# The attention output kept by feature: small transfers in place of transpositions, in a decoder block with self and cross attention

## The reference

```
x1 = LN(h);  q,k,v = x1 @ Wqkv + b;  a = softmax(causal(q k^T / 4)) v;  h = h + a @ Wp1 + b
x2 = LN(h);  q = x2 @ Wq2 + b;  k,v = ctx @ Wkv2 + b
             a = softmax(q k^T / 4 + logits[key] + mask(key > query + 2)) v;  h = h + a @ Wp2 + b
x3 = LN(h);  h = h + gelu_tanh(x3 @ Wfc + b) @ Wmlp + b          (inner width 1024)
```

## Time and profile before

| | us |
|---|---|
| median of 3 runs | 1323.19 (1321.65 to 1323.44) |
| profiled execution, its time | 1324.19 |
| profiled execution, its span | 1322.5 |
| PE busy in the span | 1116.2 (84%) |
| DVE busy | 786.8 (59%) |
| ACT busy | 614.5 (46%) |
| POOL busy | 434.6 (33%) |
| one transfer queue, share of 16 engines' span | 40.0% |
| mean granted TensorE clock | 0.933 |

### The profile page before, as it was taken

The page is one execution under the profiler, slowest core; times in us unless marked ns, Lnnn a source line. Parts: engine busy times, 40 slices in busy tenths (PEclk is TensorE's granted clock), DMA queues, the critical chain, the costliest instruction groups (busy, mean ns, idle before and its releaser), DMA issues.

```text
span 1322.5 us, 22082 instructions
## 1 busy us (share of the span) xinstructions
PE 1116.2 (84%) x7360; PEld 670.9 (51%) x7360; DVE 786.8 (59%) x1898; ACT 614.5 (46%) x1154; POOL 434.6 (33%) x805
## 2 busy tenths in 40 slices
PE   4394775888989999889989799899989999948967
PEld 2142442545455655556455555566456645534635
DVE  3471663576776677656767577667756677417513
ACT  1052242454664457444655357445744475505433
POOL 3041151243424342423524242434323243403220
PEclk9587796889999999999999899999989999988989
DMA  9406344908063543626081533626090800080000
GB/s 222 56 19 77 52 52 61 114 17 98 16 85 49 75 52 44 90 40 88 2 111 27 78 46 44 90 39 88 13 116 10 105 17 1 10 103 2 17 0 17
DMA packets 50391, 74.11 MB, mean 56 GB/s; under 512 B 6472, under 2 KB 24808, under 8 KB 50281
## 3 DMA queue, kind: packets, MB, share of 16 engines
q1 hardware_dynamic: 50281, 72.68, 40.0%
HBM read 17.45 MB, written 4.19 MB: 16 GB/s over the span
## 4 chain that ended last, share of the span: by engine, by line
PE 59%; issue 14%; DVE 10%; DMA 9%; ACT 6%; POOL 2%; SPq 1%; DVEq 0%; ACTq 0%; POOLq 0%
PE dense L515 14%; PE dense L521 12%; PE pv_out L588 10%; PE scores L574 8%; PE max_scores L556 7%; DVE row_max L789 5%; PE dense L509 3%; PE max_scores L559 3%; DMA q_stack_cross<-max_rows 3%; DMA q_stack_self<-parts_q 3%; DMA q_stack_self<-max_rows 2%; ACT probs L679 2%; DVE rest_k L822 1%; PE dense L611 1%; ACT inner L704 1%
## 5 line engine op out<-in xcount | busy, mean ns | idle before, releaser
L679 ACT ACTIVATE probs<-scores 128x512 f32<-128x512 f32 (+3 forms) x768 | 383.4, 529 | 455.7 <-PE scores L574 451.3
L789 DVE TENSOR_REDUCE row_max<-max_scores 128x1 f32<-128x512 f32 (+6 forms) x1024 | 445.6, 482 | 238.5 <-PE max_scores L559 233.9
L946 POOL TENSOR_SCALAR_AFFINE_SELECT probs<-probs 128x256 f32<-128x256 f32 x512 | 210.0, 430 | 464.1 <-ACT probs L679 463.3
L556 PE MATMUL max_scores<-k_stack_self,q_stack_self 96*128 96x512 bf16 (+3 forms) x512 | 148.7, 319 | 72.2 <-issue 56.0
L556 PE MATMUL max_scores<-k_stack_cross,q_stack_cross 99*128 99x512 bf16 (+3 forms) x512 | 145.8, 312 | 38.0 <-issue 31.7
L574 PE MATMUL scores<-q_stack_cross,k_stack_cross 101*128 101x512 bf16 (+3 forms) x512 | 135.4, 308 | 31.2 <-DMA q_stack_cross<-max_rows 19.6
L574 PE MATMUL scores<-q_stack_self,k_stack_self 98*128 98x512 bf16 (+3 forms) x512 | 137.1, 310 | 17.5 <-ACT probs L679 10.0
L521 PE MATMUL dense<-mlp_w,inner 128*128 128x256 f32 x512 | 127.7, 396 | 8.5 <-DVE rest_k L822 5.0
L515 PE MATMUL dense<-feat_b,fc_w 128*128 128x512 f32 x256 | 124.1, 610 | 3.0 <-ACT rest_k L713 1.1
L521 PEld LDWEIGHTS dense<-mlp_w,inner 128*128 128x128 f32 x512 | 97.5, 196 | 28.4 <-DVE rest_k L822 6.5
L556 PEld LDWEIGHTS max_scores<-k_stack_self,q_stack_self 96*128 96x128 bf16 x512 | 51.7, 101 | 108.9 <-issue 68.1
(11 more groups left out here) (95 smaller groups left out, 1500.7 us busy)
## 6 DMA issues: line engine op xcount, KB each, us to landing
q_stack_self<-parts_q SPq DMA_DIRECT2D x48, 256.0 KB, 9.5
k_stack_self<-parts_k SPq DMA_DIRECT2D x48, 256.0 KB, 15.5
q_stack_cross<-parts_q SPq DMA_DIRECT2D x48, 256.0 KB, 9.0
k_stack_cross<-parts_k SPq DMA_DIRECT2D x48, 256.0 KB, 12.7
x_in<-in_x SPq DMA_DIRECT2D x8, 512.0 KB, 10.7
x_in<-in_ctx SPq DMA_DIRECT2D x8, 512.0 KB, 10.4
hidden<-in_x SPq DMA_DIRECT2D x8, 512.0 KB, 13.4
out_y<-hidden SPq DMA_DIRECT2D x32, 128.0 KB, 1.7
```

The source lines that it names most:

```text
L556: pe.matmul(max_scores[:, bank, c0:c0 + W[q]], q_stack[at.kind][0:rows_, head, q * P:(q + 1) * P], k_stack[at.kind][0:rows_, head, 0:W[q]] ...
L679: nc.scalar.activation(probs[:, head % (2 * GH), c0:c0 + w], scores[:, part % EXP_BANKS, 0:w], ACT.Exp, scale=SCALE).then_inc(exp_done, 1)
L789: last = nc.vector.tensor_reduce(row_max[:, g % 2, c:c + 1], max_scores[:, part % MAX_BANKS, c0:c0 + W[q]], AX.X, ALU.max)
L946: nc.gpsimd.affine_select(out=v, in_=v, compare_op=ALU.is_ge, fill=0.0, base=q0 - kb * P + LAST[at.kind], pattern=[[0, 2], [1, P]], channe ...
```

## The change

The item `ON` becomes two. `OD` (beat 8 of a window) runs on SyncE alone: for each of the four heads one transfer brings its 16 rows of `o_turn` to their place in an `attn_out` that is now by feature, and one transfer brings its single row of sums to 16 rows of a new tile `attn_sum`. `ND` (beat 0 of the window after that, once for two groups) runs on VectorE alone: a reciprocal of 128 rows of 512 sums and a multiplication. The projections read `attn_out` directly; `ta1` and `ta2` are gone. `q` and `k` share one tile `rest`, with waits for it. The loop is gone: all iterations are written out.

```diff
-PV_AT, ON_AT, MT_AFTER = {4: (0, 1), 7: (2, 3)}, 10, 2
-BEAT = ("M", "S", "PV", "MT", "ON", "plan")
+PV_AT, OD_AT, ND_AT, MT_AFTER = {4: (0, 1), 7: (2, 3)}, 8, 0, 2
+BEAT = ("M", "S", "PV", "MT", "OD", "ND", "plan")
...
 (ta1.0, ta1.1, ta2.0, ta2.1 leave PLAN and UNUSUAL; all else keeps its beat)
...
-                elif what == "ON" and beat % GT == ON_AT:
-                    yield from fixed("ON", beat - GT)
+                elif what == "OD" and beat % GT == OD_AT:
+                    yield from fixed("OD", beat - GT)
+                elif what == "ND" and beat % GT == ND_AT and (beat - 2 * GT) // GT % 2:
+                    yield from fixed("ND", beat - 2 * GT)
...
-        attn_out = sb("attn_out", [P, TB, H])
+        attn_out = sb("attn_out", [P, HC, T])
+        attn_sum = sb("attn_sum", [P, T])
...
-        rest = {s: sb(f"rest_{s}", [P, HC, T]) for s in "qk"}
-        gelu_temp = [normed..., rest["q"][:], rest["k"][:]]
-        gelu_temp.append(gelu_temp[0])
+        rest = sb("rest", [P, HC, T])
+        gelu_temp = 2 * [normed..., rest[:]]
...
         def iterations(eng, body, after_first=None):
-            for like in range(FIRST, LOOP_FROM):
+            for like in range(FIRST, END):
                 body(like, like)
...
-            with eng.Fori(LOOP_FROM, LOOP_TO) as i:
-                body(LOOP_FROM, i)
-            for like in range(LOOP_TO, END):
-                body(like, like)
...
+                    if name == "OD":                                    # SyncE
+                        wait(sp, sum_ready["p1"], seen("p1"))
+                        wait(sp, sum_ready["p2"], seen("p2"))
+                        wait(sp, attn_ready, at.n * (NG // 2) + g // 2)
+                        sp.wait_ge(o_copied, at.n * NG + g + 1)
+                        row0 = g % 2 * (P // 2)
+                        for j in range(GH):
+                            to = slice(row0 + j * HD, row0 + (j + 1) * HD)
+                            sp.dma_start(attn_out[to, g // 2, :], o_turn[32 * j:32 * j + HD, :]).then_inc(out_moved, 16)
+                            sp.dma_start(attn_sum[to, :], o_turn[32 * j + HD:32 * j + VW, :].unsqueeze(1)
+                                         .to_broadcast([1, HD, T])).then_inc(out_moved, 16)
...
                         if part == 0:                                   # TensorE, PV
+                            wait(pe, o_copied, at.n * NG + g)
...
-                    elif name == "ON":
-                        pe.wait_ge(o_copied, at.n * NG + g + 1)
-                        for t in range(TB):
-                            last = pe.transpose(d[:, t * P:(t + 1) * P], o_turn[:, t * P:(t + 1) * P], ident[:])
...
-                        pe.wait_ge(turned["ta1" if name == "p1" else "ta2"], (b + 1) * HC)
+                        pe.wait_ge(attn_ready, (a.n + 1) * (NG // 2))
                         for t in range(2):
-                            last = by_token(d[:, t * H:(t + 1) * H], feat_b,
+                            last = by_token(d[:, t * H:(t + 1) * H], attn_out,
...
                         act.wait_ge(pv_done, at.n * NG + g + 1)         # ScalarE, PV
+                        wait(act, out_moved, (at.n * NG + g) * 2 * GH * 16)
                         nc.scalar.copy(o_turn[:], pv_out[:]).then_inc(o_copied, 1)
...
-                    elif name == "ON":                                  # VectorE
-                        nc.vector.reciprocal(recip[:, g % 2], o[:, :, :, HD]).then_inc(recip_ready, 1)
-                        nc.vector.tensor_tensor(dst..., o[:, :, :, 0:HD], recip..., ALU.mult).then_inc(attn_ready, 1)
+                    elif name == "ND":
+                        c = g // 2
+                        dve.wait_ge(out_moved, (at.n * NG + g + 1) * 2 * GH * 16)
+                        nc.vector.reciprocal(attn_sum[:], attn_sum[:]).then_inc(recip_ready, 1)
+                        dve.wait_ge(recip_ready, at.n * (NG // 2) + c + 1)
+                        nc.vector.tensor_tensor(attn_out[:, c, :], attn_out[:, c, :], attn_sum[:],
+                                                ALU.mult).then_inc(attn_ready, 1)
                     elif name in hi:                                    # VectorE, splits of q and k
...
+                        for of in lo:
+                            if of[0] != name[0]:
+                                wait(dve, lo[of], seen(of))
```

More of the change, by code:

```diff
@@ L93 @@
             46:f.6 46:G.2""",
-    "Y": """0:dq1 9:dk1 0:u.6 0:y.2 0:f.7 0:dR 2:u.7 3:G.3 5:y.3 4:R1 8:v1.0 8:v1.1 11:tc.0 12:ta1.0
-            14:tc.1 14:ta1.1 16:p1.0 17:p1.1 20:k2.0 21:k2.1 22:ma.0 24:m.0 26:tx.0 27:tx.1 29:q2.0
+    "Y": """0:dq1 9:dk1 0:u.6 0:y.2 0:f.7 0:dR 2:u.7 3:G.3 5:y.3 4:R1 8:v1.0 8:v1.1 11:tc.0
+            14:tc.1 16:p1.0 17:p1.1 20:k2.0 21:k2.1 22:ma.0 24:m.0 26:tx.0 27:tx.1 29:q2.0
             32:q2.1 35:ma.1 37:m.1 43:ma.2 45:m.2""",
@@ L191, in is_dense @@
 def is_dense(name):
-    return name not in ("M", "S", "PV", "R1", "R2", "R3", "L1", "u", "G", "y", "ma", "dR", "dq1", "dk1", "dq2", "dk2")
+    return name not in ("M", "S", "PV", "OD", "ND", "R1", "R2", "R3", "L1", "u", "G", "y", "ma", "dR", "dq1", "dk1", "dq2", "dk2")
 STARTED, BEFORE, _count = {}, {}, {}
@@ L203, with __init__ @@
             _count[_key] = _count.get(_key, 0) + 1
-PER_LOOP = BEFORE[LOOP_FROM + 1] - BEFORE[LOOP_FROM]
-assert PER_LOOP % 2 == 0
 class Seen:
-    def __init__(self, like, i):
-        self.like, self.i, self.within = like, i, {}
+    def __init__(self, like):
+        self.like, self.within = like, {}
     def after(self, name, part):
@@ L218, in __call__ @@
     def __call__(self, name):
-        n = STARTED[self.like].get(name, 0) + self.within.get(name, 0)
-        if isinstance(self.i, int):
-            return n
-        assert n > 0, name
-        return n + (self.i - LOOP_FROM) * (STARTED[LOOP_FROM + 1][name] - STARTED[LOOP_FROM][name])
+        return STARTED[self.like].get(name, 0) + self.within.get(name, 0)
 def ordered(like, i):
-    seen = Seen(like, i)
+    seen = Seen(like)
     for item in items(like, i):
@@ L306, in block_kernel @@
         o_turn = sb("o_turn", [P, T])
-        recip = sb("recip", [P, 2, TB, GH])
         stats = sb("stats", [P, TB, 6])
@@ L616, in body @@
                         last = turn(d, x_in, part)
-                    elif name in ("ta1", "ta2"):
-                        kind = "self" if name == "ta1" else "cross"
-                        a = Attn(kind, blike + (kind == "cross"), b + (kind == "cross"))
-                        pe.wait_ge(attn_ready, (a.n + 1) * NG)
-                        last = turn(d, attn_out, part)
                     elif name in ("q1", "k1"):
@@ L664, in body @@
             def body(like, i):
-                made = dense_of(like, i)
+                made = BEFORE[like]
                 for (name, part, blike, b, at, g), seen in ordered(like, i):
@@ L690, in body @@
                                              ).then_inc(turned[name], 1)
-                    elif name in ("tc", "ta1", "ta2"):
+                    elif name == "tc":
                         act.wait_ge(dense_made, made)
-                        nc.scalar.copy((feat_a if name == "tc" else feat_b)[:, part, :], d).then_inc(turned[name], 1)
+                        nc.scalar.copy(feat_a[:, part, :], d).then_inc(turned[name], 1)
                     elif name in hi:
@@ L772, in body @@
             def body(like, i):
-                made, k = dense_of(like, i), 0
+                made, k = BEFORE[like], 0
                 for (name, part, blike, b, at, g), seen in ordered(like, i):
@@ L820, in body @@
                         wait(dve, lo[other(name)], seen(other(name)))
+                        for of in lo:
+                            if of[0] != name[0]:
+                                wait(dve, lo[of], seen(of))
                         dve.wait_ge(hi[name], n)
-                        nc.vector.scalar_tensor_tensor(out=rest[name[0]][:, part, :], in0=d, scalar=column(name, part),
+                        nc.vector.scalar_tensor_tensor(out=rest[:, part, :], in0=d, scalar=column(name, part),
                                                        in1=parts[name[0]][:, 0, part, :], op0=ALU.add,
@@ L825, in body @@
                         dve.wait_ge(remains[name], n)
-                        nc.vector.tensor_copy(parts[name[0]][:, 1, part, :], rest[name[0]][:, part, :]).then_inc(mid[name], 1)
+                        nc.vector.tensor_copy(parts[name[0]][:, 1, part, :], rest[:, part, :]).then_inc(mid[name], 1)
                     elif name in v_ready:
@@ L935, in body @@
                         pool.wait_ge(mid[name], b * HC + part + 1)
-                        nc.gpsimd.tensor_tensor(parts[name[0]][:, 2, part, :], rest[name[0]][:, part, :],
+                        nc.gpsimd.tensor_tensor(parts[name[0]][:, 2, part, :], rest[:, part, :],
```

37 lines of the change are left out of this document (14 added, 23 removed), and 4 rows, old and new, of the table OFFSET.

## The result

The changed kernel takes **1504.9 us** (median of 4 runs, 1502.6 to 1509.0) where the kernel before takes 1322.5: ratio 1.138, 95% interval 1.136 to 1.141. The forecast was 1431 in a range of 1345 to 1460: the direction was right, the size was not, +182 us where +108 were forecast.

What follows compares the result with a forecast made beforehand. TensorE was taken as the pace-setter from beat 12, the transfer train before it. Slot stalls, start and end costs, less 16 us for the loop, gave +118, with overlap +108: 1431 us, range 1345 to 1460.

Steps and rivals of the forecast that it cites:

- loop: Slots X4 and X5 behind the loop's jumps: writing out all iterations removes their extra time, together -16 us.
- Y1 to Y6, X2 to X6: Middle slots: stalls for blocks and `ND`, +7.4 us a Y slot, +8.3 an X slot, +5 for Y1.
- X7 and Y7: Late slots: +8.3 us for X7 like other X slots, +5 for Y7 with its weaker train.
- start: Kernel start: first loads and reductions wait behind blocks and `ND`, 5 to 20 us, taken as 15.
- X8 and the last projection: Kernel end: block, `ND` and projections come one behind another, +12 us in X8 and +10.5 in the last projection.
- overlap: Stalls counted as if in series; a tenth of the slots' 97 us taken off.
- the reciprocal: In `ND` on VectorE: 512 elements a row take 3.5 us, making `ND` 4.25 us, 32 times.
- rival 1: VectorE's reciprocal runs at the normal pace, `ND` is 1.5 us, kernel 1355 us; chance 0.18.
- `p2.0` in X slots: X slots' projection waits for block and `ND`: +4.8 us, plus 1.7 for TensorE's lower clock.
- the clock: Y slots after beat 12: TensorE's clock is already at the 1.2 GHz level; a longer pause adds +0.5 us.
- the landing behind the train: Y slots near beat 12: the block lands 2.3 us after the train drains, 537.1 after 534.8.
- Rival 3: Eight transfers dearer behind the train, 16 copies reading one partition, SyncE block 8 us: kernel 1490 us; chance 0.06.
- Rival 2: TensorE is the bound at all times, removed transpositions count everywhere, `ND` always ends in time: 1285 us; chance 0.09.

Runs made afterwards that it cites:

- e1: The kernel before with its middle loop written out and nothing else changed: 1305.4 us, ratio 0.988.
- e4: The kernel after without VectorE's reciprocal and multiplication, all transfers kept, the projection alone waiting for their landing: 1339.8 us.
- e5: The kernel after with neither the transfers nor VectorE's step, and no wait for either: 1287.7 us.
- experiment 6: The unrolled kernel of before with the change's single rest tile, its waits and its order of the gelu pairs: 1312.1 us.
- Two by two: The kernel after without transfers 1342.7 us, without VectorE's step 1339.8, without either 1287.7, with both 1504.9.
- experiments 7, 9 and 10: The kernel after, in turn: VectorE's step three beats later, 1431.4 us; three useless matmuls at beats 16 and 40 of every slot, 1506.5; Y slots alone, 1493.7.

## Why the prediction was wrong

By its own terms, for the profiled spans (forecast, measured):

```
loop                                        -16    -16  (alone: -17)
Y1 to Y6, X2 to X6                          +83.5 +135
X7 and Y7                                   +13.3  +17
start                                       +15    +23
X8 and the last projection                  +22.5  +25
overlap                                     -10      0
sum                                        +108   +185
```

The miss is 77 us, mostly these: 4.8 us in each Y slot (12.2 against the unrolled kernel, 7.4 forecast), 4.2 in each X slot (12.5 for 8.3), 10 of overlap, and 8 in the start, which no run looks into.

- **Right.** The loop; SyncE's blocks (5.0 us, and 0.63 from one issue of 32 KB to the next, the pitch that the earlier trace rows has for 256 KB); VectorE's total (875.6, near 880); the reciprocal (3.35 us for 3.5 taken; rival 1 falls); the stalls' places; `p2.0` in X slots (beats 12 to 20 +6.8 against e1, forecast 4.8 + 1.7); X7 and Y7, X8 and the last projection (17 and 25 us for 13.3 and 22.5).
- **Wrong, the step that failed: the stalls were priced one by one and added up, with "a longer pause gives some more of it: +0.5" for the clock, 2.3 us for the landing behind the train, and 10 us taken off for overlap.** The next points take its parts in turn.
- **Wrong, the clock.** Behind two stops of TensorE (3.66 and 5.18 us in Y3) the clock stood at the lower level for 17 us, and behind a third, at beat 36, for some 7 more. Beats 12 to 20 of the Y slots grew by 7.0 us where 3.4 + 0.5 were forecast; filling the hole gave back 3.1 of it. The late landing (next point) is worth 2.3 us at the same place, so the two share an excess of 3.1 us and cannot be added. The earlier trace rows shows the level after one stop of 2.65 us, for 3.4 us in that trace; I priced only what was added to that stop, not the second stop that follows it or the work behind both that runs at half pace. As an estimate from Y3 and X3 alone, five Y and six X slots at 7.2 and 4.3 us of TensorE time come to 62 us, not all on the path.
- **Wrong, the landings.** Behind the train of Y3 4.6 us after the row maxima, not 2.3 (X3: 3.5); at beat 36 the block of Y3 ended on SyncE at 651.2 and VectorE's step started at 653.35, and from the copy (644.3) it was 9.0 us, not 8.1, while VectorE came after 6.2, not 6.7. So its wait was 2.9 us for the 1.4 that 574.8 - 573.4 gave, and beats 36 to 44 grew by 6.7, not 4.1. Without the sums' transfers the step behind the train of Y3 started 2.9 us after the row maxima (570.6 and 567.7), so 1.7 of the 2.3 us in excess are theirs. Rival 3 had the sums' transfers as a cause, but not by SyncE's 8 us; that it is the 16 copies out of one partition is not shown.
- **Wrong, the X slots' beats 7 to 12 (+1.8) and 36 to 44 (+2.8 for 2).** The previous slot's block stands on SyncE until 505.2 and the train starts behind it, at 505.93; I counted 1.2 us for this, inside `p2.0`'s 4.8. It goes with the transfers (e4 9.0, e5 10.3). Beats 20 to 31 grew by 2.3 us where 1 was taken for the common `rest` tile; experiment 6 shows 1.5 for that tile.
- **Wrong, the overlap.** I took off 10 us as if stalls hid one another. Two by two shows the contrary: alone the two parts cost 52 and 55 us, together 217. A step of 4 us on VectorE that starts on time is mostly taken up by its gaps; the same step behind a wait finds the three banks already used up, and adds its full length to the wait, and both to the low clock. That account of the 110 us is argued from the traces; experiments 7, 9 and 10 show its parts. I had the mechanism for each stall, but a sum of stalls that I then reduced has no place for what one stall does to the next.
- Rival 2 (TensorE the bound, 1285) falls for the change. 1288 with neither part, and 1285 for the old layout with the load moved, come out near the 1285 that it gave for a kernel bound by TensorE; that they are bound so was not tested.
- Slips in the working: rival 1's +39 gives 1362 us, and about 1359 with its tenth off, not 1355; and by the terms given, the block at beat 36 lands at 575.0 (568.4 + 5.1 + 1.5), not 574.8. Neither changes the forecast.

Open: what in the sums' transfers makes their landing late; where the other 0.6 us of it comes from; the 8 us in the start; and how the 110 us divide between wait and clock.

## What to carry to other kernels

A wait put at the head of an in-order engine's work and the work behind it are not two costs that add: measure each alone and both together, and put the step as many beats behind its transfer as the landing takes (74 us here). Before a stop of TensorE is priced, read how long the granted clock stays low behind the nearest such stop, and count the work that runs there. And look for a big load that stands in the queue just ahead of a small urgent transfer: moving one gave 21 us here, about as much as the removal of 96 transposition items with the VectorE work of `ON` (24).

## What the hardware showed that I had not expected

- A reciprocal on VectorE costs (3353 - 250)/(512 - 16) = 6.3 ns per element of a row, six times the 1.05 ns of a reduction, and hardly any fixed part beyond that of the others (150 ns for 145). The Trainium skill, "VectorE: DVE Perf Modes", section "First, the fixed hardware budget", has a repeat count of 8. Taken as eight times the pace of a reduction, an estimate by that page, it would be 8.4 ns; the measured ratio is 6.0.
- One transfer that writes four rows to 64 places lands 4.3 us after its issue, with only its own block ahead of it, and one that writes one row to 16 places 2.8 us. While it is alone its share of the 16 DMA engines is 0.23 to 0.24, under four engines' work. Three issues less save 1.9 us of SyncE and only 0.6 of the way from the copy to the landing (7.5 to 6.9 us), and the kernel is 43 us slower.
- Added matmuls made a kernel faster: five slots of 81.2 us became 78.0 in the profiled executions, with the granted clock back at 1.00 sooner behind the stops.
